# A four-layer gated decoder on one core: the last layer's row gathers ahead of its scatters, twelve products moved from POOL to VectorE, and the last batch summed first

## What is computed

```
scores = sigmoid(x @ gate_w.T); sfc = scores + gate_bias
# two of four groups by their two best experts, then the best 4 experts in them
_, topk_idx = top_k(where(smask, sfc, 0.0), 4)
topk_w = take(scores, topk_idx); topk_w = topk_w / (topk_w.sum(-1) + 1e-20)
combine_w = (one_hot(topk_idx, 16) * topk_w[..., None]).sum(1)
y = einsum('tei,ehi,te->th', silu(x @ gate_proj) * (x @ up_proj), down_proj, combine_w)
y = y + silu(x @ shared_gate_w.T) * (x @ shared_up_w.T) @ shared_down_w.T
x = x + tanh(g_ffn[3]) * y
```

## Time and profile before

| what | us |
|---|---|
| median of 3 runs (lowest, highest) | 2750.03 (2746.38, 2757.14) |
| the profiled execution | 2746.07 |
| its span, first to last instruction | 2744.3 |
| routing and shared expert 0 (PE 2201.7 to 2287.7) | 86.0 |
| expert blocks (2287.7 to 2669.5) | 381.8 |
| combine and shared expert 1 (2669.5 to 2744.3) | 74.8 |
| PE busy in the span | 2390.8 (87%) |
| DVE, ACT, POOL busy | 1297.3, 917.2, 678.9 |
| mean granted TensorE clock (share of 2.4 GHz) | 0.935 |

### The profile page before, as it was taken

The page is one execution under the profiler, slowest core; times in us unless marked ns, Lnnn a source line. Parts: engine busy times, 40 slices in busy tenths (PEclk is TensorE's granted clock), DMA queues, the critical chain, the costliest instruction groups (busy, mean ns, idle before and its releaser), DMA issues.

```text
span 2744.3 us, 31649 instructions
## 1 busy us (share of the span) xinstructions
PE 2390.8 (87%) x11514; PEld 1594.9 (58%) x11514; DVE 1297.3 (47%) x2735; ACT 917.2 (33%) x2049; POOL 678.9 (25%) x655
## 2 busy tenths in 40 slices
PE   6898979889779859998789988989988898888998
PEld 3455645545536647777344555544465656777774
DVE  5765256562556531110676554385545383222224
ACT  2544236452344212221365422364523121111112
POOL 3034241202202222221110021111022054344433
PEclk9988989999889879999799999999998889999999
DMA  5000000000000332221000000000000004556544
GB/s 217 1 1 1 0 1 1 1 1 1 0 8 1 134 113 100 98 97 41 29 16 1 1 0 1 1 1 1 1 1 17 9 23 167 185 198 203 186 145 151
DMA packets 46939, 147.69 MB, mean 54 GB/s; under 512 B 5776, under 2 KB 30480, under 8 KB 38736
## 3 DMA queue, kind: packets, MB, share of 16 engines
q1 hardware_dynamic: 35392, 114.87, 11.9%
q0 software_dynamic: 11424, 31.21, 3.6%
HBM read 119.84 MB, written 26.21 MB: 53 GB/s over the span
## 4 chain that ended last, share of the span: by engine, by line
PE 68%; DVE 16%; DMA 5%; ACT 4%; issue 4%; POOL 3%; ACTq 0%; DVEq 0%; POOLq 0%; SPq 0%
PE PS L587 6%; PE PS L993 6%; PE PS L984 6%; PE PS L2102 5%; PE PS L2116 5%; DMA arena<-slots,from_row 4%; PE PS L617 4%; PE PS L2392 4%; PE PS L2406 3%; PE PS L528 3%; PE PS L943 3%; PE PS L567 3%; DVE arena L691 2%; PE PS L774 2%; PE PS L1188 2%
## 5 line engine op out<-in xcount | busy, mean ns | idle before, releaser
L648 ACT ACTIVATE arena<-PS,arena 128x512 f32<-128x512 f32 (+3 forms) x512 | 306.2, 605 | 206.2 <-DVE arena L691 173.0
L691 DVE TENSOR_REDUCE arena<-PS 128x1 f32<-128x512 f32 (+3 forms) x512 | 273.0, 583 | 137.6 <-PE PS L593 84.6
L587 PE MATMUL PS<-arena 64*128 64x512 f32 (+3 forms) x1024 | 293.9, 567 | 30.9 <-ACT arena L648 20.3
L299 POOL TENSOR_TENSOR arena<-arena 128x4 f32<-128x4 f32 x41 | 47.0, 1146 | 759.6 <-DVE arena L310 445.8
L2392 PE MATMUL PS<-arena 128*128 128x256 f32 (+2 forms) x1128 | 216.0, 348 | 0.9 <-DVE arena L2437 0.9
L2392 PEld LDWEIGHTS PS<-arena 128*128 128x128 f32 (+1 forms) x1128 | 182.7, 183 | 29.2 <-issue 1.3
L617 PE MATMUL PS<-arena 128*128 128x128 f32 x1280 | 174.0, 281 | 15.4 <-ACT arena L648 12.8
L587 PEld LDWEIGHTS PS<-arena 64*128 64x128 f32 x1024 | 104.2, 187 | 142.1 <-ACT arena L648 92.3
L872 POOL TENSOR_TENSOR arena<-arena 128x512 f32<-128x512 f32 (+2 forms) x108 | 88.8, 825 | 381.9 <-ACT arena L843 376.2
L617 PEld LDWEIGHTS PS<-arena 128*128 128x128 f32 x1280 | 140.3, 143 | 70.5 <-ACT arena L648 48.0
L984 PE MATMUL PS<-arena 128*128 128x512 f32 x384 | 168.0, 594 | 3.1 <-ACT arena L1001 3.1
(11 more groups left out here) (397 smaller groups left out, 3990.4 us busy)
## 6 DMA issues: line engine op xcount, KB each, us to landing
arena<-e SPq DMA_DIRECT2D x49, 1088.0 KB, 5.3
arena<-e SPq DMA_DIRECT2D x8, 2048.0 KB, 9.0
arena<-yslots SPq DMA_DIRECT2D x22, 512.0 KB, 8.3
arena<-w3a SPq DMA_DIRECT2D x1, 4106.0 KB, 12.2
yslots<-zeros SPq DMA_DIRECT2D x1, 4096.0 KB, 31.7
arena<-w3b SPq DMA_DIRECT2D x1, 3593.0 KB, 20.2
arena<-w0a SPq DMA_DIRECT2D x1, 2054.0 KB, 13.0
arena<-w0f SPq DMA_DIRECT2D x1, 2052.0 KB, 20.2
```

The source lines that it names most:

```text
L587: ins = nc.tensor.matmul(PS[:, hh, 0:w], q[:, t * P:(t + 1) * P], k[:, 0:w], start=True, stop=not cfg["causal"])
L648: nc.scalar.activation(PRB[m % 6][:, 0:w], PS[:, hh, 0:w], ACT.Exp, bias=nmax[:, m:m + 1], accum_out=rsum[:, col:col + 1]).then_inc(s["pro ...
L691: nc.vector.tensor_reduce(nmax[:, m:m + 1], PS[:, hh, 0:w], AX, ALU.max, negate=True).then_inc(s["nmax"], 1)
```

## The change

There are three edits.

1. In the loop over the blocks POOL issues `rows(j + 3)` ahead of `store(j)`. The waits of both stay what they were.
2. The twelve products of shared expert 0 leave POOL. `dve_mix3(v, m)` makes product m on VectorE, reading the up product straight from its bank, and the calls stand between the steps of the routing chain. ACT's twelve copies of up into `ups3` go away for this expert. The bank of an up product is now free when VectorE has multiplied, so PE's gate product m waits for `mixed` of product m-2, where it waited for ACT's copy. The large one-hot comparison is cut into two halves so that a product can stand between them. `downs3` has eight slots in place of four for the first expert, and so ACT's scaled copy waits for an addition two batches back. The second expert keeps its products on POOL.
3. Loads and combine go in the order 3, 0, 1, 2 (`ORDER3`). POOL's last four additions wait for the combine of batch 3 alone, and batch 3 leaves in four DMAs of one tile each, every one as soon as its tile is added.

The core of the diff:

```diff
-        def dve_take(ch, val, picks, tops, e, signal=None):
+        def dve_take(ch, val, picks, tops, e, signal=None, beside=None):
...
+                if beside is not None and k < len(picks) - 1:
+                    beside(k)
...
-        def dve_onehots3(ch, lows, highs, low, high, n, nh, signal):
+        def dve_onehots3(v, ch, lows, highs, low, high, n, nh, signal):
 
             V = nc.vector
+            dve_mix3(v, 6)
             ch.link(V.tensor_tensor(highs[:, :, 1, :], high.unsqueeze(2).to_broadcast([P, n, nh]),
                                     counting[:, 0:nh].unsqueeze(1).to_broadcast([P, n, nh]), ALU.is_equal))
+            dve_mix3(v, 7)
             ch.link(V.tensor_tensor(highs[:, :, 0, :], highs[:, :, 1, :],
                                     counting[:, 1:n + 1].unsqueeze(2).to_broadcast([P, n, nh]), ALU.mult))
+            dve_mix3(v, 8)
             V.tensor_scalar(highs[:, :, 1, :], highs[:, :, 1, :], lane_f, None, ALU.mult)
-            V.tensor_tensor(lows, low.unsqueeze(2).to_broadcast([P, n, P]),
-                            counting.unsqueeze(1).to_broadcast([P, n, P]), ALU.is_equal).then_inc(signal, 1)
+            for h in range(2):
+                part = slice(h * n // 2, (h + 1) * n // 2)
+                ins = V.tensor_tensor(lows[:, part], low[:, part].unsqueeze(2).to_broadcast([P, n // 2, P]),
+                                      counting.unsqueeze(1).to_broadcast([P, n // 2, P]), ALU.is_equal)
+                if h:
+                    ins.then_inc(signal, 1)
+                else:
+                    dve_mix3(v, 9)
+            dve_mix3(v, 10)
+            dve_mix3(v, 11)
...
+            dve_mix3(v, 0)
+            dve_take(ch, sfc, [onehot[:, k] for k in range(TOPK3)], TOPK3 * [top], E3, None, lambda k: dve_mix3(v, k + 1))
...
+            dve_mix3(v, 4)
...
+            dve_mix3(v, 5)
...
-        ups3 = [region("kv", 22816 + i * T, T) for i in range(2)]
-        downs3 = [region("kv", 23840 + t * C, C) for t in range(QT)]
+        ups3 = [region("kv", 23840 + i * T, T) for i in range(2)]
+        downs3 = [region("kv", 22816 + t * C, C) for t in range(2 * QT)]
+
+        def down3(it, t):
+            return downs3[it % 2 * QT + t if it < B else t]
...
-                    j = it * 6 + 2 * c + up
-                    if j >= 3:
-                        pe.wait_ge(s["up_out"], j - 2)
+                    j, m = it * 6 + 2 * c + up, it * 3 + c
+                    if up and m:
+                        pe.wait_ge(s["gate_out"], m)
+                    elif m >= B * 3 + 2:
+                        pe.wait_ge(s["up_out"], m - (B * 3 + 1))
+                    elif m >= 2:
+                        pe.wait_ge(s["mixed"], m - 1)
...
-                nc.scalar.activation(mixed3[it % 2][c][0:n, :], PS[0:n, (2 * c) % 3, :], ACT.Silu).then_inc(s["up_out"], 1)
+                nc.scalar.activation(mixed3[it % 2][c][0:n, :], PS[0:n, (2 * c) % 3, :], ACT.Silu).then_inc(s["gate_out"], 1)
+                if it < B:
+                    return
+                if it == B and c == 0:
+                    act.wait_ge(s["added"], B * QT)
...
-                    if it:
+                    if it > B:
                         act.wait_ge(s["added"], (it - 1) * QT + t + 1)
-                    nc.scalar.activation(downs3[t], PS[:, 4 + t, 0:C], ACT.Copy, scale=tg[:, 7:8]).then_inc(s["down_out"], 1)
+                    elif it > 1:
+                        act.wait_ge(s["added"], (it - 2) * QT + t + 1)
+                    nc.scalar.activation(down3(it, t), PS[:, 4 + t, 0:C], ACT.Copy, scale=tg[:, 7:8]).then_inc(s["down_out"], 1)
...
+        def dve_mix3(v, m):
+            it, c = divmod(m, 3)
+            n = IC3[c]
+            v.wait_ge(s3m["gate_out"], m + 1)
+            v.wait_ge(s3m["up_psum"], 2 * m + 2)
+            to = mixed3[it % 2][c][0:n, :]
+            nc.vector.tensor_tensor(to, to, PS[0:n, (2 * c + 1) % 3, :], ALU.mult).then_inc(s3m["mixed"], 1)
...
-                pool_mix3(pool, it, 0)
+                if i:
+                    pool_mix3(pool, it, 0)
                 if b:
                     pool_add3(pool, it - 1)
-                pool_mix3(pool, it, 1)
-                pool_mix3(pool, it, 2)
+                if i:
+                    pool_mix3(pool, it, 1)
+                    pool_mix3(pool, it, 2)
...
+        ORDER3 = (3, 0, 1, 2)
...
-            for q in range(B):
+            for q in ORDER3:
...
-            for q in range(B):
+            for n, q in enumerate(ORDER3):
...
-                            v.wait_ge(s["summed"], q * TOPK3 + k)
+                            v.wait_ge(s["summed"], n * TOPK3 + k)
...
             for j in range(NB3):
-                store(j)
                 if j + 3 < NB3:
                     rows(j + 3)
+                store(j)
...
-                pool.wait_ge(s["summed"], B * TOPK3)
+                pool.wait_ge(s["summed"], TOPK3)
...
-            for q in range(B):
-                if q < B - 1:
-                    sp.wait_ge(s3m["summed"], (q + 1) * TOPK3)
-                else:
-                    sp.wait_ge(s3m["added"], 2 * B * QT)
+            for n, q in enumerate(ORDER3[1:]):
+                sp.wait_ge(s3m["summed"], (n + 2) * TOPK3)
                 sp.dma_start(out[q * T:(q + 1) * T, :].rearrange("(t p) c -> p t c", p=P), X[:, q * QT:(q + 1) * QT, :]
                              ).then_inc(ld["stored"], 16)
-            sp.wait_ge(ld["stored"], B * 16)
+            for t in range(NT - QT, NT):
+                sp.wait_ge(s3m["added"], NT + t + 1)
+                sp.dma_start(out[t * P:(t + 1) * P, :], X[:, t, :]).then_inc(ld["stored"], 16)
+            sp.wait_ge(ld["stored"], (B - 1 + QT) * 16)
 
         @block.gpsimd
         def _(pool):
```

More of the change, by code:

```diff
@@ L1626, in program @@
         s3m = sems("l3moe", "sig tables table_psum slots x0 x1 x2 w0 w1 w2 xT_psum xT copied y0_stored y1_stored "
-                   "y2_stored back3 wa act_in dve_in hidden o_psum extra up_psum up_out mixed down down_out added summed")
+                   "y2_stored back3 wa act_in dve_in hidden o_psum extra up_psum gate_out up_out mixed down down_out added summed")
         gtile = hT.rearrange("p a n -> p (a n)")
@@ L1919, in dve_route3 @@
             top = temp(NT)
-            dve_take(ch, sfc, [onehot[:, k] for k in range(TOPK3)], TOPK3 * [top], E3)
+            dve_mix3(v, 0)
+            dve_take(ch, sfc, [onehot[:, k] for k in range(TOPK3)], TOPK3 * [top], E3, None, lambda k: dve_mix3(v, k + 1))
             V.tensor_scalar(chosen3.rearrange("p (t e) -> p t e", e=E3), sfc, NEG / 2, None, ALU.is_lt).then_inc(s["tables"], 1)
@@ L1993, in dve_route3 @@
             ch.link(V.scalar_tensor_tensor(out=low, in0=high, scalar=-float(P), in1=slot, op0=ALU.mult, op1=ALU.add))
-            dve_onehots3(ch, low3, high3, low, high, nseg, HI3, s["tables"])
+            dve_onehots3(v, ch, low3, high3, low, high, nseg, HI3, s["tables"])
             pair, row_, extra = temp(NB3), temp(NB3), temp(NB3)
@@ L2304, in pool_add3 @@
                 xt = X[:, it % B * QT + t, :]
-                nc.gpsimd.tensor_tensor(xt, xt, downs3[t], ALU.add).then_inc(s3m["added"], 1)
+                nc.gpsimd.tensor_tensor(xt, xt, down3(it, t), ALU.add).then_inc(s3m["added"], 1)
         def pool_shared3(pool, i, last):
```

2 lines of the change are left out of this document (1 added, 1 removed).

## The result

The changed kernel runs in 2678.73 us (median of 4 runs, 2675.49 to 2681.22), the kernel before in 2748.20 us beside it (4 runs, 2744.12 to 2757.14). The ratio is 0.9742, with a 95% interval of 0.9715 to 0.9769. The profiled execution took 2680.02 us, its span is 2678.2 us, and before it was 2746.07 and 2744.3 us.

What follows compares the result with a forecast made beforehand. PE was busiest, but late row gathers set the block loop's period, VectorE's chain bounded routing, and the end waited for VectorE. Gains of 48.2 + 1.5 + 5.2 = 54.9 us gave 2691.2 profiled, 2695 us median; range 2685 to 2712.

Steps and rivals of the forecast that it cites:

- from the profiled execution to the median: Whole kernel: the profiled execution lay 4.0 us under the median of the runs shown, so 2691.2 became 2695 us.
- POOL's additions in edit 2: Routing stage: twelve additions staying on POOL still cost VectorE 0.4 us each, so 4.9 us of its excess stays.
- a round of 20.83 us: Block loop: without gather waits PE becomes the bound, rounds falling from 24.18 to 20.83 us; 43.6 us over 13 rounds.
- 50 as an upper end: Block stage: upper end of the 48.2 us gain, if rounds can be a little shorter still; the lower end was 36.
- Edit 2: 1.5 us forecast: Routing stage: moving products to VectorE gains 10.1 - 7.8 - 0.1 - 0.7 = 1.5 us; ends 5 lost and 5 gained.
- The excess of 15.0 us: Routing stage: VectorE's instructions stretched beside POOL's 12 products and 12 additions add up to 15.0 us, estimated by comparing forms.
- Edit 3: 5.2 forecast: Last stage: POOL's last additions wait for ACT instead of the combine, gaining 5.2 us; ends 3 and 6.
- the smaller last output DMA: End of the last stage: the last output DMA is a quarter as large, put at 0.2 us gained.
- (a): Block loop: a new wait replaces the gather's once a round, gaining 13 us in place of 48; 2730 us, chance 0.06.
- (b): Routing: VectorE and PE hold each other up, losing 6.8 us instead of gaining 1.5; 2703 us, chance 0.09.
- (c): Block loop: PE falls to its lower clock, making the kernel slower; 2885 us with all fifteen rounds, chance 0.02.
- (d): Block loop: gathers land late because of DMA engines, not their place; only 6.7 us gained, 2743 us, chance 0.03.

Runs made afterwards that it cites:

- the kernel with the first gather alone: The changed kernel with one more wait: SP loads the second and third blocks' weights only after the first block's gather has landed; 2672.63 us, ratio 0.9739.

## Why the prediction was wrong, and where it was right

The direction, the mechanisms and the place of each gain were right, and the time was 16.3 us too high. What failed are sizes of terms. The forecast added 4.0 us from the profiled execution to the median, where 1.3 were to be taken off, and its range allowed 4 us for run-to-run shift, where executions of the kernel before lie 22 us apart. It kept 4.9 us for POOL's additions in edit 2, which cost 1.4. And it took a round of 20.83 us, which takes 20.61. By its own steps:

1. **Rounds of the block loop: 20.83 us taken, 20.61 measured.** The failure is the choice of the clean round. I took PE's busy time in a round between two waits. Such a round holds two things that a round without waits does not. At its start the down product begins 0.49 us after the transposes and not 0.44. At its end the last gate and up products count whole, where in a steady round the next transposes begin 0.16 us before these products end (2311.18 and 5.34 against 2316.36 above). Over 13 rounds the 0.22 us are 2.9 us. The first gate and up products were 0.85 shorter (7.17 for 8.02), and that is not edit 1's: with edit 1 alone they took 8.07 us, with edit 2 alone 6.96, and they vary from 6.85 to 8.24 over all the profiles. The stage gained 51.9, where I had 48.2 and 50 as an upper end. The rest of this part held: no wait but the first, clock 1.00, down products of 2.76 us, landings within their room, PE the bound.
2. **Edit 2: 1.5 us forecast, 5.1 measured** (4.9 between the means of the whole kernels, 86.1 and 81.2, the one with the whole comparison left out). The excess of 15.0 us was right. The additions, 4.9 us in my sum, cost 2.0 before (15.0 less 13.0) and 1.4 after. The products cost 0.61 and not 0.65 each, 0.5 us in all, and the waits for PE 1.3 and not 0.7. The chain from its first instruction to from_row3 shortened by 76.0 - 71.0 = 5.0. The first gather landed about as late as before. It was the upper end of that term.
3. **Edit 3: 5.2 forecast, 5.05 measured.** VectorE combined batches 3 and 0 in one stretch of 19.71 us, slower than the 15.59 for two batches before, and the room I had seen was enough. The 0.2 us for the smaller last output DMA did not come: from the end of POOL's last addition to the end of the span it is 4.74 us before and 4.73 after.
4. **4.0 us ahead of the changed stages**, booked by nobody. It is chance: this start lies between 2189.7 and 2201.7 in profiles of the kernel before alone.
5. **From the profiled execution to the median: 4.0 added, 1.3 to be taken off.** I carried the distance of one profiled execution from the median of three runs over to another kernel. It was no property of profiles. That is 5.3 us.

3.7 + 3.6 - 0.15 + 4.0 + 5.3 is 16.5, the miss but for rounding. More than half of it, items 4 and 5, is run-to-run spread. The range gave 4 us for that, and the runs of the kernel before turned out to cover 22. Without this spread the time would have been 2688 us, inside the range; so the miss of the range is in part bad luck, while the terms of the change were still 7 us short. A low end at 2678 or less would have been in order even with the terms as they were. One slip is in the high end: a third of (a) with (b) is 2715 by their own numbers, not 2712.

**The rivals.** (a), a new wait once a round, and (c), PE at its lower clock in the loop, did not come. (d) is refuted by the kernel with only the second block's gather moved. (b), VectorE and PE holding each other up, is real, and one instruction's split decides it: 0.87 and 0.46 us of waits with it, 4.93 without. I had judged it by the one wait of the earlier trace rows and had not seen that the split was the remedy.

## What to carry to other kernels

Where an in-order queue serves several blocks of a loop, find the one block whose request comes late; moving only that one brought all 50 us here. Take the clean round's length from the starts of two rounds without a wait, since PE's busy time between two waits holds an end that otherwise overlaps what follows, and count the granted clock's loss behind waits with the waits themselves. When work moves to the engine that bounds a stage, its place between long instructions can be worth more than its length: here half of a comparison later or earlier was 4 us, the product itself 0.6.

## What the runs showed of the hardware that I had not expected

Fourteen waits, 36.1 us in all, had cost 11.1 us of PE's own time too, in down products alone, and in two other kernels with the same waits the block stage was 8 to 10 us longer at a granted clock of 0.93 and 0.94.

The blocking between POOL and VectorE is lopsided where VectorE's instruction is the long one: a 0.72 us addition took 9.17 us beside a 9.20 us comparison of VectorE, while VectorE's 5.42 us instructions grew by 0.46 and 0.34 with additions beside them.

The DMA engines moved 427 GB/s when full; in the first two microseconds of that all of it, and in the next two 86%, came through the queue of the weight loads, out of device memory. The Trainium skill, DMA: Bandwidth & Descriptors, section Where 436 GB/s comes from, gives 435 for the way into SBUF, with which this agrees, and about 358 for one core's half of that memory's rate; this kernel ran on one core, and the measurement is above that half. A gather of two tiles landed 8.0 us after its first issue where two weight loads of 1088 KB were issued in the 1.7 us ahead of it and two more before its second DMA; with one such load ahead of it, it landed after 4.6 us (2267.15 to 2271.70 in the kernel with the first gather alone).
